# A graph layer's second row of masks: from DRAM to every partition, or made on ScalarE from the first

## The reference

```python
z2 = concatenate([node_feat[src], node_feat[dst], edge_feat], -1)
e = relu(z2 @ W_pre + b_pre)                  # one row of 128 per edge
s, mean_sq = segment_sum(e, dst), segment_sum(e * e, dst)
mx, mn = segment_max(e, dst), segment_min(e, dst)
# mean, mx, mn and std, scaled three ways by the degree, then two dense layers,
# residual and layer norm
x = layernorm(x + first_layer)
x = layernorm(x + second_layer(x))            # GCN and GAT convolutions on the same edges
```

## Time and profile before

| | us |
|---|---|
| median of three runs | 7348.3 |
| profiled execution, its span | 7200.7 |
| median less that span | 147.6 |
| TensorE busy | 5306.6 |
| VectorE busy | 4043.0 |
| GpSimd busy | 3792.6 |
| ScalarE busy | 2988.5 |

### The profile page before, as it was taken

The page is one execution under the profiler, slowest core; times in us unless marked ns, Lnnn a source line. Parts: engine busy times, 40 slices in busy tenths (PEclk is TensorE's granted clock), DMA queues, the critical chain, the costliest instruction groups (busy, mean ns, idle before and its releaser), DMA issues. The chain is left out here.

```text
span 7200.7 us, 135903 instructions
## 1 busy us (share of the span) xinstructions
PE 5306.6 (74%) x31642; PEld 4026.1 (56%) x31642; DVE 4043.0 (56%) x12632; ACT 2988.5 (42%) x8170; POOL 3792.6 (53%) x3867
## 2 busy tenths in 40 slices
PE   4777777777777777785888786677777777777774
PEld 3555555555555555543666664566666666566664
DVE  5656656665666666665555555455455555455557
ACT  2444444444444444423666664233333333333335
POOL 3555555555555555502555551666666666666662
PEclk7888888888888888896888886555555555555555
DMA  5433333433334333332111111222222222222222
GB/s 158 106 99 101 100 99 99 102 103 99 101 102 105 100 99 103 100 95 57 39 39 38 38 39 26 44 44 43 44 43 44 44 44 44 44 43 44 43 44 46
DMA packets 531406, 504.25 MB, mean 70 GB/s; under 512 B 328647, under 2 KB 390672, under 8 KB 531023
## 3 DMA queue, kind: packets, MB, share of 16 engines
q0 software_dynamic: 122832, 255.14, 15.7%
q1 hardware_dynamic: 337654, 130.31, 8.6%
q10 hardware_dynamic: 70794, 117.58, 4.9%
HBM read 476.98 MB, written 25.63 MB: 70 GB/s over the span
## 5 line engine op out<-in xcount | busy, mean ns | idle before, releaser
L604 POOL DMA_INDIRECT G<-Atab,ms x1616 | 1577.2, 976 | 1411.2 <-DVE EE L627 523.5
L1840 POOL DMA_INDIRECT Gt<-TAB,metat x1632 | 1606.2, 984 | 1067.2 <-issue 454.6
L1304 POOL DMA_INDIRECT Gc<-XS,metac x560 | 542.1, 968 | 500.9 <-PE Sc L1495 233.4
L2010 PE MATMUL SR<-P,Gt 128*128 128x64 f32 x3264 | 803.8, 428 | 0.0
L701 ACT COPY BS<-BK 128x512 f32<-128x512 f32 x808 | 436.2, 588 | 872.0 <-remote 855.7
L2010 PEld LDWEIGHTS SR<-P,Gt 128*128 128x128 f32 x3264 | 727.1, 328 | 47.8
L1882 DVE TENSOR_REDUCE lt<-MT 128x1 f32<-128x256 f32 x408 | 170.2, 417 | 978.1 <-DMA WB<-Btab 958.2
L662 DVE TENSOR_TENSOR acc<-acc,TT 128x64 f32 (+1 forms) x808 | 178.4, 233 | 862.8 <-remote 534.9
L1998 PE MATMUL PT<-ident,EX 128*128 128x128 f32 x816 | 269.5, 434 | 520.3 <-ACT EX L1960 481.9
L805 PE MATMUL SX<-BS,oh 128*32 128x256 f32 x3232 | 564.7, 475 | 69.6 <-issue 47.3
L754 PE MATMUL SS<-EE,oh 128*32 128x256 f32 x3232 | 571.5, 465 | 48.4 <-issue 46.8
(11 more groups left out here) (288 smaller groups left out, 10615.3 us busy)
## 6 DMA issues: line engine op xcount, KB each, us to landing
mm<-MM ACTq DMA_DIRECT2D x202, 512.0 KB
ZR<-in_eft SPq DMA_DIRECT2D x202, 256.0 KB
Gt<-TAB,metat POOLq DMA_INDIRECT x1632
tb<-DF SPq DMA_DIRECT2D x202, 128.0 KB
G<-Atab,ms POOLq DMA_INDIRECT x1616
dq<-DQ SPq DMA_DIRECT2D x12, 768.0 KB, 5.9
Gc<-XS,metac POOLq DMA_INDIRECT x560
ad<-ADT SPq DMA_DIRECT2D x408, 0.5 KB
```

Of the source, the lines that this page charges most:

```text
L604: e.indirect_dma_start(G[:, k, s, :], None, Atab, bass.IndirectOffsetOnAxis(ap=ms[:, k, s:s + 1], axis=0)).then_inc(l_g[k], 16)
L1304: e.indirect_dma_start(G[:, k, s, :], None, XS, bass.IndirectOffsetOnAxis(ap=meta[:, k, s:s + 1], axis=0)).then_inc(l_g[k], 16)
L1840: e.indirect_dma_start(G[:, k, s, :], None, TAB, bass.IndirectOffsetOnAxis(ap=meta[:, k, s:s + 1], axis=0)).then_inc(l_g[k], 16)
L2010: m = e.matmul(SR[q][:, 0:2 * W], G[:, k, s, 0:128], P[:, q, s * 2 * W:(s + 1) * 2 * W], start=(s == 0), stop=(s == 3))
```

## The change

Only row 0 is loaded to all partitions, into `mkb`: 256 KB for two chunks. A new function `resets` on ScalarE makes the other row, `rsb`, for one chunk in each round: Identity(-1e30 x mask + 1e30), which is 0 where the mask is 1 and 1e30 where it is 0. The bias is a column `bigb`, filled once by VectorE. A new semaphore `s_rs` counts these. VectorE's scans wait for it and no longer for the DMA. In ScalarE's list `masks` moves from lag 2 to lag 1, and `resets` stands at lag 3 behind `half`. The wait of `masks` on `s_d3` keeps its form, so in a round it now asks for a scan one chunk younger than before.

```diff
--- before.py
+++ after.py
@@ -499,7 +499,9 @@
         ZR = sbt(ph, "ZR", [128, 4, CH])
         WB = sbt(ph, "WB", [128, 4, 128])
         dstb = tb[:, :].bitcast(F32).rearrange("p (a n) -> p a n", a=4)
-        mm2 = sbt(ph, "mm2", [128, 2, 2, 2 * CH], BF16)
+        mkb = sbt(ph, "mkb", [128, 2, 2 * CH], BF16)
+        rsb = sbt(ph, "rsb", [128, 2, 2 * CH], BF16)
+        bigb = sbt(ph, "bigb", [128, 1])
         G = sbt(ph, "G", [128, 4, 4, 128])
         EE = sbt(ph, "EE", [128, 4, 2, CH])
         oh = sbt(ph, "oh", [128, 4, 8, W])
@@ -542,6 +544,7 @@
         s_d4a = sem("l_d4a")
         s_d4b = sem("l_d4b")
         s_i = sem("l_i")
+        s_rs = sem("l_rs")
         s_pool = v["s_pool"]
         s_pad = v["s_pad"]
         s_sync = v["s_sync"]
@@ -612,6 +615,7 @@
             e.memset(SN[:, :, :, :], 0.0).then_inc(s_i, 1)
             halves = ident[:, :].rearrange("p (a h n) -> p a h n", a=2, h=2)
             e.tensor_tensor(I2[:, :, :], halves[:, :, 0, :], halves[:, :, 1, :], ALU.add).then_inc(s_i, 1)
+            e.memset(bigb[:, :], BIG).then_inc(s_i, 1)
             e.wait_ge(s_i, 3)
             T = load_T(e, tb, 0)
 
@@ -640,12 +644,12 @@
             def d3(j):
                 k, q = j.slot(4), j.slot(2)
                 wait(e, s_p2t, j.at(1))
-                wait_pair(e, l_m, j, 16)
+                wait(e, s_rs, j.at(1))
                 if not j.first(1):
                     wait(e, s_d3, j.at())
-                e.tensor_tensor_scan(ST[:, q, 0, :], mm2[:, k // 2, 0, ds(k % 2 * CH, CH)], ET[q][:, :], ST[:, 1 - q, 0, CH - 1:CH],
+                e.tensor_tensor_scan(ST[:, q, 0, :], mkb[:, k // 2, ds(k % 2 * CH, CH)], ET[q][:, :], ST[:, 1 - q, 0, CH - 1:CH],
                                      ALU.mult, ALU.max)
-                e.tensor_tensor_scan(ST[:, q, 1, :], mm2[:, k // 2, 1, ds(k % 2 * CH, CH)], ET[q][:, :], ST[:, 1 - q, 1, CH - 1:CH],
+                e.tensor_tensor_scan(ST[:, q, 1, :], rsb[:, k // 2, ds(k % 2 * CH, CH)], ET[q][:, :], ST[:, 1 - q, 1, CH - 1:CH],
                                      ALU.max, ALU.min).then_inc(s_d3, 1)
 
             regs = [e.alloc_register(f"l_base{k}") for k in range(4)]
@@ -693,7 +697,15 @@
                 if not j.first(4):
                     wait(e, s_d3, j.at(-2))
                     e.sem_inc(s_pad, 1)
-                e.dma_start(mm2[:, r, :, :], MM[:, ds(c * CH, 2 * CH)].partition_broadcast(128)).then_inc(l_m[r], 16)
+                e.dma_start(mkb[:, r, :], MM[0, ds(c * CH, 2 * CH)].partition_broadcast(128)).then_inc(l_m[r], 16)
+
+            def resets(j):
+                k = j.slot(4)
+                wait_pair(e, l_m, j, 16)
+                if j.first(1):
+                    e.wait_ge(s_i, 4)
+                e.activation(rsb[:, k // 2, ds(k % 2 * CH, CH)], mkb[:, k // 2, ds(k % 2 * CH, CH)], ACT.Identity,
+                             scale=-BIG, bias=bigb[:, 0:1]).then_inc(s_rs, 1)
 
             def back(j, a):
                 q = j.slot(2)
@@ -723,7 +735,7 @@
                 p = slice(2 * (1 - q) * W, 2 * (2 - q) * W)
                 e.copy(SN[p, q, :, :], SX[p, 0:256].rearrange("p (a n) -> p a n", a=2)).then_inc(s_e2, 1)
 
-            pipeline(e, T, U, D, [(5, e1), (2, a1), (2, masks), (3, half), (5, a2a), (5, a2b), (6, e2)])
+            pipeline(e, T, U, D, [(5, e1), (2, a1), (1, masks), (3, half), (3, resets), (5, a2a), (5, a2b), (6, e2)])
 
         @blk.tensor
         def _(e):
```

## The result

Four timed runs of each: the medians are 7398.8 us with the change and 7352.9 before. The ratio is 1.0058, with a 95% interval of 1.0033 to 1.0083. The change costs 0.58%, 43 us (the two medians alone differ by 46), or 0.21 us in each of the 202 pairs. The forecast was 117 us faster.

The account below looks back on a forecast made before the run. No engine is full in the first layer; waits in freezes cost 4.48 us a pair, 905 us in all. Relief of -242 and price of +125 give -117: 7348.3 to 7231 us, with 8 in 10 within 7010 to 7490.

Parts of the forecast that it names:

- Less stacked bursts: First layer: mask loads halved and farther from edge-feature loads shorten the freezes (engines standing still), -242 us over 202 pairs.
- The reading of the bins: Pairs sorted by time from mask load to edge-feature load: 2 to 4 us took 13.5 us, under 0.6 took 14.9.
- the bin above 4 us: The 16 pairs with over 4 us between loads took 17.9 us, explained as the long pair delaying the second load.
- rival B: Freezes have nothing to do with the mask load, so only ScalarE's new queue is paid: 7473 us, chance 0.36.
- The other term: ScalarE's wait for the younger scan and the activation before the BS copies: +125 us, from 66 and 59.
- In pairs without a freeze: VectorE's addition comes 1.9 us late behind ScalarE's queue, paid in 35 of 202 pairs: 66 us.
- the bound of +529 us: Upper bound of the cost: 202 pairs at 2.62 us from scan to copies, if no freeze covers any.
- In pairs that freeze: In 167 pairs the freeze covers the scan wait; half the 0.71 us activation before the copies counts, 59 us.
- The sign named in advance: Forecast holds if ScalarE's and VectorE's "remote" waits, with no instruction found ending just then, fall well over 125 us.
- the likeliest range: Whole kernel at 7056 to 7340 us, from relief between 158 and 350 and price between 60 and 150.
- the landing of the load: The mask load has two rounds to land before the activation asks for it, so it costs nothing.
- ScalarE's amount of work: With the activation, 3.96 us of work in a round of at least 5.12 us, so not the bound by amount.

Follow-up runs that it names:

- e1_lag1_only: The kernel before with only the mask load moved to lag 1, still 512 KB and without the activation: 1.0058 of before.
- e8: The kernel before with one of the four indirect gathers of each first-layer chunk, output wrong: 0.8297 of before, 6107.7 us.
- e6_no_loads: The kernel before with masks zeroed once and each pair's mask load cut to one partition, 4 KB instead of 512: 1.0003 of before.
- e14: The changed kernel with one of the four gathers of each chunk: 0.9320 of before, 6834.5 us.
- e0_before_again: The kernel before, unchanged, profiled a second time: 0.9998 of before, span 7334.8 us.
- e7: The changed kernel with masks back at lag 2 and the activation at the end of ScalarE's round, behind the copies: 1.0002 of before.
- e17: The changed kernel with masks at lag 2, the activation at the end of ScalarE's round and one of four gathers a chunk: 0.8292 of before, 6068.4 us.

## Why the prediction was wrong

The step that failed is "Less stacked bursts are thus worth some 14.72 - 13.5 = 1.2 us a pair", the term of -242 us. Measured, it is nothing: 1.0006 with half the load and 1.0003 with 4 KB in its place, and no gain in e1_lag1_only, where all pairs have the greater distance. The freezes came with the gathers (e8). The reading of the bins had cause and effect the wrong way round. In the first profile, 31 of the 54 pairs with 2 to 4 us between the two loads have no "remote" wait before `BS` at all, and 21 of the 76 with 1.2 to 2 us. Pairs without one take 11.72 and 11.69 us in these two bins, pairs with one 15.87 and 15.86: at the same number of freezes the distance changes nothing. And in e6_no_loads, where the mask load is 4 KB, the same sorting still gives 14.6 us for the 56 pairs with 2 to 4 us and 15.4 for the 34 with 0.6 to 1.2. I had seen such a reversal in the bin above 4 us and explained it away there, but trusted the bin below it., a stage without such loads that still has 626.8 us of such waits, was the better witness. That was rival B.

The other term was of the right kind, but mis-sized. The cost was put at +125 us, so B gives 7473, and the whole measured 43 us. Its two parts:

- *In pairs without a freeze*, 1.9 us was forecast and 3.7 us measured where no pair freezes. The chain was as told; missing was the lower clock of TensorE behind the gap, 1.5 us more from SX to the end of TT. So the bound of +529 us, for no freeze that covers any of it, was too low: e14 costs some 750. The count was wrong too: 157 waits are not 157 pairs. Of the 189 pairs of the first profile 54 have no such wait, 115 have one and 20 have more, so 54 pairs were open to the cost, and not 33.
- *In pairs that freeze*, half an activation, 0.35 us, was forecast. Over all pairs 0.21 us is left, though more pairs were open to the cost, at a higher price, than I took. At 1.9 us the 54 pairs alone would be over 100 us, so more is covered than the sum allows, and some of it in pairs that I counted as open. The traces show quick rounds getting fewer: 97 of 367 rounds of e0_before_again take under 5.5 us from one first scan to the next, and 70 of 365 with the change. How the 43 us divide among the pairs was not settled.

The sign named in advance misled as well. ScalarE's and VectorE's "remote" waits together fell from 1327.9 to 557.7 us (from 1200.3, by e0_before_again), "well over 125 us", and the kernel was slower. The same waiting is now listed before `ohb` and as a wait for TensorE's `TT`. The whole idle time in front of an instruction was the thing to compare. Two smaller slips change nothing: 12 of the 24 pairs "with under 0.6 us" had their edge features before the mask load, and the lower end of the likeliest range, from 350 and 60, is 7058 and not 7056.

What was right: the landing of the load and the first scan are not on the path; ScalarE's amount of work costs nothing that can be measured (e7, e17); VectorE has nothing much to wait for before its scans, 15.6 us against 8.5 in all. The time is inside the stated range, but only because the range reached to rival B. The parts do not add while the freezes are there (0.58, 0.54 and together 0.58%); without them 2.65 and 0.54 give 3.69 together, more than their sum. The likely reason for the first is that the freezes hide what is in their time, the same for one delay or for two; only the sums were measured.

## What to carry to other kernels

A correlation over the rounds of one trace does not say which of two transfers that start together causes a stall, or whether the stall moved them. Load one of them to one partition instead of 128, which keeps every wait, and see. A wait that is gone from its line can stand at the next one under another name: compare the whole idle time. New work on an in-order engine is priced by what stands behind it: the same 0.72 us activation cost 0.54% before two copies and nothing behind them. And a cost hidden under another stall comes back when that stall is gone, here 43 us against some 750.

## What the runs showed of the hardware that was not expected

- One indirect gather in four instead of all removed every freeze of TensorE's issue and of the engines that wait for it in 200 to 1800 us; the kernel took 0.83 of the time. A quarter of the bytes with all gathers changed nothing (0.9992). What in the gathers stalls the others was not settled.
- Mask loads move 99.95 MB in 200 to 3000 us, some 35% of all that DMA moves there (101 GB/s by the earlier trace rows); cutting them to one partition changed the time by 0.03%, inside the interval.
- TensorE was idle for 2.72 us at a granted clock of 1.00 and was put to 0.50 only once it worked again, with BK at 1.97 us instead of 1.09 (e14).
- The unchanged kernel ran at medians of 7185 to 7355 us on different chips.
